# A head's outputs in two banks in turn, copied after the third rounding and summed after the last maximum, in the first half of a decoder kernel

## The reference

```
x = layernorm(x + attention(x, Wq, Wk, Wv, Wo))     # 32 query heads, 8 kv heads, head size 64, rope, causal
x = layernorm(x + quantized_cross_part(x, fside, ctx))
x = layernorm(x + ffn(x, up_w, down_w, scales))      # sign of the weights, hidden size 2048, relu
```

```
attn = einsum('bkgqd,bkld->bkgql', q, k) * SCALE
p    = softmax(where(causal, attn, -inf))
out  = einsum('bkgql,bkld->bkgqd', p, v)
y    = out.reshape(B, L, 2048) @ Wo.T
```

## Time and profile before

| | before |
|---|---|
| median of 3 runs | 1364.2 us (1364.01 to 1366.48) |
| the profiled execution | 1364.12 us, span 1362.3 us |
| TensorE busy | 1282.2 us (94%) |
| VectorE, ScalarE, GpSimd busy | 981.4, 914.5, 783.9 us |
| mean granted clock of TensorE | 0.99 |
| first half, its 64 heads | about 38.8 to 545.6 us of the span |

### The profile page before, as it was taken

The page is one execution under the profiler, slowest core; times in us unless marked ns, Lnnn a source line. Parts: engine busy times, 40 slices in busy tenths (PEclk is TensorE's granted clock), DMA queues, the critical chain, the costliest instruction groups (busy, mean ns, idle before and its releaser), DMA issues.

```text
span 1362.3 us, 25175 instructions
## 1 busy us (share of the span) xinstructions
PE 1282.2 (94%) x7112; PEld 1068.6 (78%) x7112; DVE 981.4 (72%) x2453; ACT 914.5 (67%) x2160; POOL 783.9 (58%) x690
## 2 busy tenths in 40 slices
PE   5899999999999999999999999999997999999996
PEld 3788888888888877888888887888776676777885
DVE  3677777777767776888987888778986778865322
ACT  3676677776777776777677877777667775555432
POOL 4555565655556576655775557586651264746454
PEclk9999999999999999999999999999999999999998
DMA  4722222222222223333223222322223602100000
GB/s 147 232 64 55 63 54 69 59 67 63 68 66 72 63 56 93 86 93 86 63 71 78 55 71 55 93 57 68 65 57 115 247 17 77 47 16 31 1 31 31
DMA packets 55285, 98.78 MB, mean 73 GB/s; under 512 B 11792, under 2 KB 13840, under 8 KB 54288
## 3 DMA queue, kind: packets, MB, share of 16 engines
q1 hardware_dynamic: 55184, 97.57, 25.7%
HBM read 51.39 MB, written 4.19 MB: 41 GB/s over the span
## 4 chain that ended last, share of the span: by engine, by line
PE 71%; DVE 10%; issue 8%; ACT 6%; POOL 3%; DMA 1%; SPq 0%; DVEq 0%; ACTq 0%; POOLq 0%
PE m L1929 17%; PE m L1901 10%; PE ps_s L1901 8%; PE m L2203 8%; PE ps_o L1963 7%; PE ps_t L1951 7%; PE ps_s L2222 4%; PE ps_t L2222 4%; DVE probs L1544 2%; ACT probs L1305 2%; PE m L1973 2%; DVE pT_lo L1615 2%; ACT pT_hi L1313 2%; DVE o_sum L1552 1%; POOL o_lo L1121 1%
## 5 line engine op out<-in xcount | busy, mean ns | idle before, releaser
L1305 ACT ACTIVATE probs<-probs,neg_max 128x128 f32<-128x128 f32 (+3 forms) x512 | 284.9, 558 | 146.9 <-DVE neg_max L1544 146.3
L1615 DVE TENSOR_TENSOR pT_lo<-ps_t,pT_hi 128x512 fp32r<-128x512 f32 (+1 forms) x384 | 220.9, 596 | 152.1 <-ACT pT_hi L1313 149.7
L1544 DVE CUSTOM_DVE_ANT_0 probs<-ps_s,mask 128x128 f32<-128x128 f32 (+3 forms) x512 | 228.3, 482 | 9.7 <-PE ps_s L1901 9.6
L1901 PE MATMUL ps_s<-k_st,q_st 128*128 128x256 f32 (+2 forms) x1024 | 230.4, 347 | 3.2 <-DMA q_st<-q_tmp 3.0
L1951 PE MATMUL ps_t<-ident,probs 128*128 128x128 f32 x1280 | 184.7, 275 | 34.6 <-ACT probs L1305 17.5
L1121 POOL TENSOR_TENSOR o_lo<-o_sum,o_hi 128x512 fp32r<-128x512 f32 x64 | 82.0, 1282 | 202.2 <-ACT o_hi L1327 202.0
L1951 PEld LDWEIGHTS ps_t<-ident,probs 128*128 128x128 f32 x1280 | 146.9, 140 | 61.1 <-DVE pT_lo L1615 26.2
L1313 ACT ACTIVATE pT_hi<-ps_t 128x512 fp32r<-128x512 f32 (+1 forms) x384 | 186.2, 520 | 12.1 <-PE ps_t L1951 9.2
L1963 PE MATMUL ps_o<-pT_hi,v_st 128*128 128x256 f32 (+2 forms) x512 | 169.0, 341 | 0.0
L1963 PE MATMUL ps_o<-pT_lo,v_st 128*128 128x256 f32 (+2 forms) x512 | 156.2, 327 | 0.0
L1901 PEld LDWEIGHTS ps_s<-k_st,q_st 128*128 128x128 f32 x1024 | 151.3, 191 | 6.2 <-issue 3.4
(11 more groups left out here) (267 smaller groups left out, 3045.3 us busy)
## 6 DMA issues: line engine op xcount, KB each, us to landing
q_st<-q_tmp SPq DMA_DIRECT2D x512, 64.0 KB, 2.0
raw<-in_wq_t SPq DMA_DIRECT2D x32, 256.0 KB, 3.0
k_st<-k_st SPq DMA_DIRECT2D x64, 128.0 KB, 2.3
raw<-in_wo_t SPq DMA_DIRECT2D x32, 256.0 KB, 3.0
raw_b<-in_ffn_t SPq DMA_DIRECT2D x10, 512.0 KB, 7.1
raw<-in_wkv_t SPq DMA_DIRECT2D x16, 256.0 KB, 3.6
y<-in_x SPq DMA_DIRECT2D x4, 1024.0 KB, 7.6
w_gu<-in_fside_t SPq DMA_DIRECT2D x4, 1024.0 KB, 6.0
```

What stands on the lines that cost most here:

```text
L1305: act.activation(probs[:, h % 2, SO[i]:SO[i] + SW[i]], probs[:, h % 2, SO[i]:SO[i] + SW[i]], ACT.Exp, bias=neg_max[:, h % 2, i:i + 1], sca ...
L1544: dve.tensor_tensor_reduce(out=probs[:, h % 2, SO[i]:SO[i] + SW[i]], in0=ps_s[:, i % 2, 0:SW[i]], in1=mask[:, L - SW[i]:L], scale=-SCALE, ...
L1615: dve.tensor_tensor(pT_lo[:, d, :], ps_t[:, (h + k) % 2, 0:P * w].rearrange("p (w c) -> p w c", c=P), f32(pT_hi[:, d, :]), ALU.subtract).t ...
L1901: i = pe.matmul(dst, a, c, start=(j == 0), stop=(j == len(terms) - 1))
```

## The change

In the first half the outputs of even heads stay in `ps_o` and those of odd heads go to `pc`. ScalarE's copy of head n - 1 moves from the start of head n to behind `high_p` 2 of head n, ahead of `high_q` and of `exp` 2 and 3. VectorE's sum moves from behind maximum 1 to behind maximum 3. `values(n)` now waits for the sum of head n - 2 and no longer for that of head n - 1. In the second half all stays in place, but for the first head there, whose copy and sum read the bank in which the last head of the first half lies.

```diff
+        def out_bank(half, h):
+
+            return pc if half == 0 and h % 2 == 1 else ps_o
...
-            def copy_o(n, h):
+            def copy_o(n, h, half):
                 act.wait_ge(pv, n + 1)
                 wait(act, o_added, n - 1)
                 a, c = (0, HD) if h % 2 == 0 else (HD, 0)
-                act.activation(o_part[a:a + HD, :], ps_o[c:c + HD, :], ACT.Copy).then_inc(o_copied, 1)
+                act.activation(o_part[a:a + HD, :], out_bank(half, h)[c:c + HD, :], ACT.Copy).then_inc(o_copied, 1)
...
-                        if prev or h > 0:
-                            copy_o(n - 1, (h - 1) % G)
+                        if half == 1:
+                            copy_o(n - 1, (h - 1) % G, 0 if is_step(g, HKV) and (b, h) == (0, 0) else 1)
                         high_p(n, h, 0)
                         high_p(n, h, 1)
...
                         high_p(n, h, 2)
+                        if half == 0 and (prev or h > 0):
+                            copy_o(n - 1, (h - 1) % G, 0)
                         if h == 1 and nxt:
                             high_q(u + 1, (0, 1))
...
-                            if k == 0 and (prev or h > 0):
-                                add_o(n - 1, (h - 1) % G, u * 2 + (h - 1) // 2)
+                            if k == 0 and half == 1:
+                                add_o(n - 1, (h - 1) % G, u * 2 + (h - 1) // 2, 0 if is_step(g, HKV) and (b, h) == (0, 0) else 1)
                         if more:
                             softmax_max(n + 1, (h + 1) % 2, 2)
                             softmax_max(n + 1, (h + 1) % 2, 3)
+                        if half == 0 and (prev or h > 0):
+                            add_o(n - 1, (h - 1) % G, u * 2 + (h - 1) // 2, 0)
...
-            def values(n, h, buf):
-
-                wait(pe, o_added, n)
+            def values(n, h, buf, half):
+                wait(pe, o_added, n - 1 if half == 0 else n)
...
-                        i = pe.matmul(ps_o[:, q0:L], v_st[:, buf, kt, v0:v0 + P], pT[:, blocks, :],
+                        i = pe.matmul(out_bank(half, h)[:, q0:L], v_st[:, buf, kt, v0:v0 + P], pT[:, blocks, :],
```

More of the change, by code:

```diff
@@ L1510, in _ @@
             steps(act, body)
-            copy_o(U * G - 1, 3)
+            copy_o(U * G - 1, 3, 1)
             later("act0", SLOTS)
@@ L1546, in softmax_max, with add_o @@
                                          op1=ALU.min, accum_out=neg_max[:, h % 2, i:i + 1]).then_inc(maxed, 1)
-            def add_o(n, h, q):
+            def add_o(n, h, q, half):
                 dve.wait_ge(o_copied, n + 1)
@@ L1551, in add_o @@
                 a = HD * (h % 2)
-                dve.tensor_tensor(o_sum[a:a + HD, :], ps_o[a:a + HD, :], o_part[a:a + HD, :], ALU.add).then_inc(o_added, 1)
+                dve.tensor_tensor(o_sum[a:a + HD, :], out_bank(half, h)[a:a + HD, :], o_part[a:a + HD, :], ALU.add).then_inc(o_added, 1)
             def normalize(g, b, p):
@@ L1888, in _ @@
             steps(dve, body)
-            add_o(U * G - 1, 3, U * 2 - 1)
+            add_o(U * G - 1, 3, U * 2 - 1, 1)
             dve.wait_ge(m1_full, m1_fill(STEPS, 0, "out3"))
@@ L2065, in body @@
                             later("pe3", slot(g, b, h))
-                        values(n, h, b % 2)
+                        values(n, h, b % 2, half)
             def spread(dst, src, n):
```

## The result

The changed kernel took 1368.14 us in the median of 12 runs (1363.51 to 1370.03), the kernel before 1364.11 us (12 runs, 1361.21 to 1366.48) beside it. The ratio is 1.002 with a 95% interval of [1.0011, 1.003]: slower by some 2.7 us by this ratio (4.0 us by the medians), where I had forecast 0.65 us less and a range up to 1366.0 us. A second set of runs on one chip gave 1366.33 against 1365.5 us, ratio 1.0009 [0.9998, 1.002], an interval that just includes no change. Both medians of the changed kernel lie above my range.

The account below looks back on a forecast made before the run. TensorE bounds the kernel, busy 473.7 of 496 us in the first-half stretch. Terms: 1.6 lost - 1.6 - 0.65 won = -0.65 us, from 1364.12 to 1363.5 us; range 1361.5 to 1366.0 us.

Parts of the forecast that it names:

- b = 0, h = 1: Head 1 (heads count from 0) in unit 0 of a step: the copy stays ahead of the last exponentials; 1.6 us lost.
- my allowance of 0.1 us: First rounding inside the hardware loop: up to 0.1 us later than +0.64, for the waits' register values.
- the sum: VectorE's sum behind the last maximum: maxima come earlier by about its 0.69 us, add_y stays within 0.1 us; cost 0.
- The idle time before `normalize` that I took for cover: VectorE's waits for TensorE before normalize, 18.6 us in 22 cases, 0.85 us each, would cover the rest of the delay.
- my third rival: Sum in front of add_y delays the reciprocals' transposes at up to 23 places: 9 us slower, 1373 us; chance 0.03.
- b = 1, h = 1: Head 1 (heads count from 0) in unit 1 of a step, 8 heads: 1.2 to 2.0 us won, taken as 1.6.
- The stall at T01: TensorE's idle time at the eight transposes opening the head behind b = 1, h = 1: grows from 0.63 to about 1.0.
- ScalarE's wait in front of the second `high_q`: Wait for GpSimd's rotate_q, 0.62 us in b = 1, h = 1: would stay, at 8 or 9 times.
- The first unit: Unit without output projection: stalls at the k = 2 transposes of heads 2 and 3 shrink; 0.65 us won, at worst 0.4.
- The bank: Second bank for the outputs of values: worth nothing by itself, only permits the copy and the sum to stand later.

Follow-up runs that it names:

- kernel with the late projection: Changed kernel, with TensorE's output projection piece in b = 0, h = 1 of the first half moved behind scores 2 and 3 and vT: ratio 1.0005.
- late sum: Changed kernel, with VectorE's sum one place further back, behind add_y and the reciprocal: 1364.81 us, ratio 1.0001.

## Why the prediction was wrong, point by point

**The step that failed, b = 0, h = 1**: "In the loop `high_p(0)` moves from +1.13 to +0.64, which wins 0.49 and pays 0.62". The first rounding did move to +0.64, in the loop too, so my allowance of 0.1 us wasn't needed. But not all of this win reaches the copy, for there is a third rounding between, which waits for T2. ScalarE in the changed kernel, step 5, T01 at 361.82, which answers to the earlier trace rows:

```profile
362.46 1.08 ACT L1317 ACTIVATE pT_hi<-ps_t 128x512 fp32r<-128x512 f32 x2
...
364.85 0.50 ACT L1309 ACTIVATE probs<-probs,neg_max 128x256 f32<-128x256 f32 x1
...
365.64 0.38 ACT L1317 ACTIVATE pT_hi<-ps_t 128x256 fp32r<-128x256 f32 x1 [0.19 <-PE ps_t L1959]
366.05 0.59 ACT L1324 ACTIVATE o_part<-ps_o 64x512 f32<-64x512 f32 x1
...
368.19 0.71 ACT L1309 ACTIVATE probs<-probs,neg_max 128x512 f32<-128x512 f32 x1
```

and TensorE, which answers to the earlier trace rows:

```profile
361.82 1.03 PE L1959 MATMUL ps_t<-ident,probs 128*128 128x128 f32 x8
...
363.73 0.50 PE L1909 MATMUL m<-woT_hi,o_hi 128*128 128x512 f32 x1 [0.40 <-POOL o_lo L1125]
...
365.23 0.38 PE L1959 MATMUL ps_t<-ident,probs 128*128 128x128 f32 x2
...
369.05 0.77 PE L1959 MATMUL ps_t<-ident,probs 128*128 128x128 f32 x5 [0.76 <-ACT probs L1309]
```

and T2 and the third rounding of the kernel before, whose T01 is at 360.05:

```profile
363.43 0.38 PE L1951 MATMUL ps_t<-ident,probs 128*128 128x128 f32 x2
...
364.07 0.38 ACT L1313 ACTIVATE pT_hi<-ps_t 128x256 fp32r<-128x256 f32 x1
```

T2 comes 3.41 us after T01 in the changed kernel, behind the projection and its wait for `o_lo`, and ends at 365.61; the rounding starts at 365.64 with 0.19 us of idle time before it. The rounding stood at +4.02 before and stands at +3.82, so of the 0.49 us only 0.20 are won. Against the copy's 0.62 us this gives 0.4; measured were 0.36 in the loop and 0.43 and 0.38 us in steps 6 and 0. In step 7 GpSimd did cover the copy, which costs nothing there; that head is 0.08 us shorter, but so it is with the sum alone moved (7.49 us in both kernels, 7.57 before), so the copy didn't win it. The sum is 5 x 0.36 + 0.43 + 0.38 - 0.08 = 2.5 us instead of 1.6. The kernel with the late projection takes T2 out of the way and gives 0.08 instead of 0.36. That T2 held the rounding is shown.

**The other step that failed, and the larger in size, the sum**: "The maxima before it come earlier by about the same, because `pT_lo` and the maxima run back to back today, so `add_y` stays within 0.1 us of its place". They run back to back before because the sum fills what would be a wait for the same third rounding. VectorE in the changed kernel, step 5, b = 0, h = 0, T01 at 353.36:

```profile
356.92 0.42 DVE L1621 TENSOR_TENSOR pT_lo<-ps_t,pT_hi 128x256 fp32r<-128x256 f32 x1 [0.44 <-ACT pT_hi L1317]
357.26 0.55 DVE L1550 CUSTOM_DVE_ANT_0 probs<-ps_s,mask 128x384 f32<-128x384 f32 x1
...
358.46 0.70 DVE L1558 TENSOR_TENSOR o_sum<-pc,o_part 64x512 f32<-64x512 f32 x1
359.18 0.69 DVE L1573 TENSOR_TENSOR y<-y,m 128x512 f32<-128x512 f32 x1
...
360.88 0.69 DVE L1564 TENSOR_TENSOR o_sum<-o_sum,m 128x512 f32<-128x512 f32 x1 [0.91 <-PE m L1980]
```

The kernel before in the same place, T01 at 351.74, and the transposes of the reciprocals in both kernels:

```profile
356.20 0.55 DVE L1544 CUSTOM_DVE_ANT_0 probs<-ps_s,mask 128x384 f32<-128x384 f32 x1
...
357.28 0.68 DVE L1567 TENSOR_TENSOR y<-y,m 128x512 f32<-128x512 f32 x1
...
358.31 0.60 PE L1973 MATMUL m<-ident,r_rep 128*128 128x128 f32 x4
...
360.04 0.65 PE L1980 MATMUL m<-ident,r_rep 128*128 128x128 f32 x4
```

The maxima did move up, the third by 0.56 us (3.90 us after T01, 4.46 before), but the sum takes 0.12 + 0.72 us, so `add_y` starts 5.82 us after T01 instead of 5.54. Before, the transposes of the reciprocals started 0.35 us after its end (358.31); now they start at 360.04, 0.17 us after its end. That is how long TensorE takes when it has to wait: the kernel with the sum moved alone shows 0.16 to 0.18 us here too. So only some 0.18 us of room had been there. In the heads 2 of steps 1 to 5 it was less: 0.16 to 0.19 us after the end before, 0.13 us now. There `add_y` comes only some 0.1 us later (5.88 against 5.78 us after T01), about what I had named, and these heads are still 0.10 and 0.12 us longer. In steps 1 to 6 each head 2 and the head 0 of b = 0 pays 0.05 to 0.16 us, which with 0.06 us in one head of step 0 is 2.2 us in all, where I had put 0. The idle time before `normalize` that I took for cover is still there, 16.7 us in 22 cases in the stretch of the earlier trace rows; it lies behind the place that was hit, since `normalize` waits for the very transposes that wait for `add_y`. It was my third rival in a small form. Without the earlier rounding it would have been nearly that rival in full: 1.0057, some 7.8 us, with the sum moved alone. That the late sum gives 8.31, 8.39 and 8.37 us shows the cause.

**b = 1, h = 1 was right.** The stall moved from T2 to T01, and GpSimd sets the head. TensorE, T01 of head 0 at 386.76, answering to the earlier trace rows:

```profile
393.68 1.03 PE L1959 MATMUL ps_t<-ident,probs 128*128 128x128 f32 x8
396.03 0.44 PE L1959 MATMUL ps_t<-ident,probs 128*128 128x128 f32 x2 [0.34 <-DVE pT_lo L1621]
400.69 1.09 PE L1959 MATMUL ps_t<-ident,probs 128*128 128x128 f32 x8 [0.73 <-ACT probs L1309]
```

From one head 0 to the head 2 behind it now takes 13.93 us instead of 14.18: 0.25 us won in the loop, my upper value, and 0.15 to 0.20 outside; 1.8 us in all against 1.6 forecast. The copy's move is what wins it: with the sum moved alone the two heads take 14.18 us. The details I gave for it were off. T2 keeps 0.34 us of idle time instead of 0.1, since `high_o` held the first rounding to +0.75 in that head (394.43); `high_o` itself had waited 0.32 us for `normalize`, where I had said that it would be no later. The stall at T01 is 0.73 us instead of 1.0. ScalarE's wait in front of the second `high_q` is gone in steps 1 to 5 (4 of 9 cases are left in the first half), where I had it stay, since the copy now stands in that time. GpSimd sets the head all the same: in step 5 its second rotation ends at 398.67 and `high_q` starts at 398.70, and in the kernel with the copy behind the fourth exponential the wait is back (5.6 us, 9 times) while the head stays at 7.01 us. **The first unit was right**: 0.34 + 0.27 = 0.61 us against 0.65. **The bank was right**: no gain. The Trainium skill's rule (Perfetto Trace Analysis, section Matmuls), by which matmul groups should rotate through banks, gave no time in this case: the kernel with the bank alone measured 1.0002.

The terms together: 2.5 + 2.2 - 1.8 - 0.6 = +2.3 us counted in the heads, against 1.6 + 0 - 1.6 - 0.65 = -0.65. Of the 3 us between the two, the sum's place is 2.2 us and the copy in b = 0, h = 1 is 0.9 us. Beyond that, my range was narrow for the clock, which moved single runs of one kernel by 6 us, while I had gone by three runs of before. What stays open is why the first set of runs of the changed kernel lies 1 us above the second at equal mean clock, and what makes the clock fall at 520 to 540 us in one execution and not in another.

## What to carry to other kernels

When an instruction moves past others in a queue, follow the win through every one of them: an instruction between, which waits for another engine, cuts the win off, while the cost of what was moved behind it is paid in full. An engine that runs "back to back" may do so because the instruction to be moved fills a wait, so ask what the next one waits for once it is gone. A copy or sum that nobody needs soon belonged, in this kernel, behind the last instruction that TensorE waits for: behind the fourth exponential and behind `add_y` (0.9971 of before, and 0.9955 with the projection behind T2). Where waits are too small for a view of waits, the lengths of the repeated heads showed them.

## What the runs showed of the hardware that I had not expected

The whole time of one and the same kernel moved by 6 us, mostly with the mean granted clock: the changed kernel took 1363.2 to 1363.7 us in its four runs at 0.993 and 1366.5 to 1369.7 us in its eight runs at 0.989. The mean lengths of its heads at full clock agreed to 0.02 us in its two profiled executions. One profiled execution hid a loss of 2.3 us behind 2.5 us of clock.

Where TensorE had to wait for `add_y`, its transposes started 0.13 to 0.17 us after the end of `add_y` in the hardware loop of the changed kernel, and 0.06 us after it in step 6, which is written out.
